# Attention and a rounded feed-forward block on one core: contexts 2 and 3 get a second place, the first weight unit comes in halves, zeros are multiplied at the top, and every engine's order is new

## The chip, the cores and the metric

The kernel runs on one core of a Trainium2 chip. The metric is the device time of one execution in microseconds. Before the change the median of three runs is 617.62 us (617.29 to 618.58).

## What is computed

There are 4 batches of 512 rows with 512 features each, and a context of 512 rows with 256 features for each batch. Attention weights are made of the context alone, and are applied to the layer-normed rows along their 512 features. Then a gated feed-forward block with 2048 hidden features follows, whose operands are rounded to FP8 values in blocks of 32 with a scale of their own.

```python
query = einsum('bnc,dc->bnd', ctx, Wq) + bq            # 4 x 512 x 128
key   = einsum('bnc,dc->bnd', ctx, Wk) + bk
attention = softmax(einsum('bnd,bmd->bnm', query, key))
x = x + einsum('bln,bmn->blm', layernorm(x), attention)
n = mx(layernorm(x))                                   # mx: per block of 32, scale * fp8(value / scale)
hidden = silu(n @ mx(gate_w).T) * (n @ mx(up_w).T)     # 2048 x 2048
x = x + mx(hidden) @ mx(down_w).T
```

## The kernel before

The kernel is written with one hand-ordered list of calls for each engine and semaphores between them. Sizes are cut as follows: the 2048 rows are 16 row tiles r of 128 (four to a batch b), the hidden features are 4 chunks c of 512, and the weights are 12 units u of 128x2048 floats. Units 2c and 2c+1 are gate and up of chunk c; units 8 to 11 are the down weights.

**Attention of a batch b.** `project(b, 0)` and `project(b, 1)` (L654) make query and key, four matmul records each. ScalarE copies them out (`take_projection`, L901). `energies(b, 0..3)` (L661) make the scores, VectorE takes each row's maximum (`row_max`, L1369), ScalarE the exponential (`exponential`, L927), VectorE the reciprocal of the sums (`row_sum`, L1374), ScalarE makes four diagonal matrices of them (`weigh`, L935). `turn_probs(b, 0..3)` (L668) turns and weighs the probabilities, ScalarE copies them out (`take_probs`, L942), `attend(b, 0..3)` (L677) applies them, and VectorE adds them to the rows (`add_attended`, L1386).

**Rows and weights.** VectorE and ScalarE round each unit and each batch of rows: `unit_reduce`, `unit_largest`, `unit_scale`, `unit_power`, `unit_magnitude` (ScalarE, L870), `unit_round` (two passes, L1350 and L1351) and `unit_dequant`, about five passes of 128x2048 on VectorE in all. The result is written as a high and a low half-precision part: `unit_hi` on ScalarE, a DMA of GpSimd that adds the high part to the negated value (`unit_rest`), `unit_lo` on ScalarE. Each part is turned by a DMA on SyncE's queue (`turn_unit_hi`, `turn_unit_lo`). Both parts lie in one buffer each, so a unit's part waits until that of the unit before is turned. The rows of a batch go the same way (`center`, `rows_scale`, `rows_round`, `rows_dequant`, `rows_hi`, `rows_lo`), and later each hidden row tile.

**Products.** `product(r, c)` (L693) needs the parts of units 2c and 2c+1 and those of its batch's rows: 24 matmuls, each 128x512. ScalarE applies silu to the gate (`silu_of`, L1000), VectorE multiplies (`hidden_of`, L1503). `down(r)` (L705, L708) is 48 matmuls. TensorE does 16 attends, 64 products and 16 downs, in an order given by its list and by the table `products`.

**Memory.** The table `bank_uses` says in which order each of the eight PSUM banks serves the results (p, e, t, a, g, u, d for projection, energies, turned, attended, gate, up, down): a result waits until its bank's former use is copied out. Before the change, contexts 2 and 3 are loaded over contexts 0 and 1 (`ctx[b % 2]`), so their loads wait for the projections. Centered rows of batch 0 go to `early_xw`, a slot of `h` that nothing uses before.

**SyncE's queue** issues the loads and the turning DMAs one after the other; a wait in it holds all that stand behind. Unit u+3 is loaded into the buffer of unit u once `unit_lo(u)` is done.

## Time and profile before

| | |
|---|---|
| median of three runs | 617.62 us |
| profiled execution, its own time | 618.75 us |
| its span | 617.0 us |
| TensorE busy | 599.0 us, 97% of the span |
| VectorE busy | 495.3 us, 80% |
| ScalarE busy | 301.9 us, 49% |
| first matmul | 8.46 us after the span's start |
| last matmul ends | about 613.1 us |

The profiled execution is 1.1 us above the median, and 1.75 us of its time lie around its span. A busy figure is the union of an engine's instructions; matmuls are pipelined, so a short gap between two groups can be hidden in it. The profile's granted clock is 1.00 in every slice but the last.

### The profile page before, as it was taken

Reading aid. Unit: us, or ns where it says so; the run is one execution under the profiler, and the core shown is the slowest. Engines: PE = TensorE matmul, PEld = TensorE weight load, DVE = VectorE, ACT = ScalarE, POOL = GpSimd, SP = SyncE. Lnnn points to the kernel's source line nnn. Section 1 sums busy time; section 2 is a strip of 40 time slices with the busy share of each in tenths; the row PEclk is TensorE's granted clock in tenths of the full one; section 3 lists DMA queues with packets and bytes.
Section 4 is the critical chain, followed back from the end, with each engine's and each line's share of the span. In section 5 each row is a group of like instructions: output and inputs, shape, how many; then the busy total and the mean of one; then the engine's idle time right before and its main releaser. Section 6 shows DMA issues by size and latency. Waiting matters only on the chain.

```text
span 617.0 us, 7089 instructions
## 1 busy us (share of the span) xinstructions
PE 599.0 (97%) x2624; PEld 276.9 (45%) x2624; DVE 495.3 (80%) x467; ACT 301.9 (49%) x449; POOL 42.4 (7%) x58
## 2 busy tenths in 40 slices
PE   4899989999999999999999999999999999999997
PEld 1535455444444444444444444444444444444443
DVE  5899999998999998996999999520149999999810
ACT  1899995645554545465455564502114232643420
POOL 1000000201000000101001110000000000010100
PEclk9999999999999999999999999999999999999999
DMA  8927769798987885968847758605000002777771
GB/s 336 410 76 168 223 191 261 176 266 211 204 223 199 209 211 141 217 120 170 205 95 155 158 110 185 119 1 85 1 1 1 2 0 37 134 122 134 122 135 34
DMA packets 147586, 90.18 MB, mean 146 GB/s; under 512 B 134240, under 2 KB 134368, under 8 KB 142816
## 3 DMA queue, kind: packets, MB, share of 16 engines
q1 hardware_dynamic: 142368, 63.78, 43.2%
q0 software_dynamic: 5184, 25.95, 18.7%
q8 instruction: 21, 0.34, 0.2%
q14 instruction: 13, 0.11, 0.0%
HBM read 25.76 MB, written 8.39 MB: 55 GB/s over the span
## 4 chain that ended last, share of the span: by engine, by line
PE 89%; ACT 6%; SPq 2%; DMA 2%; issue 1%; DVEq 0%; DVE 0%; ACTq 0%
PE bank L693 53%; PE bank L705 18%; PE bank L708 9%; PE bank L677 4%; PE bank L654 2%; ACT h L915 1%; PE bank L668 1%; ACT h L906 1%; PE bank L661 1%; DMA gu_hi<-in_ctxT 1%; SPq L377 1%; DMA xT<-hT 1%; ACT mag L870 1%; ACT hT L961 0%; ACT dn L927 0%
## 5 line engine op out<-in xcount | busy, mean ns | idle before, releaser
L693 PE MATMUL bank<-gu_hi,xT 128*128 128x512 f16 x1024 | 243.2, 379 | 0.4 <-DMA xT<-hT 0.4
L693 PEld LDWEIGHTS bank<-gu_hi,xT 128*128 128x128 f16 x1024 | 100.0, 98 | 121.8 <-DMA xT<-hT 1.1
L693 PE MATMUL bank<-gu_lo,xT 128*128 128x512 f16 x512 | 131.4, 379 | 0.0
L705 PE MATMUL bank<-dn,hT 128*128 128x512 f16 x512 | 113.1, 379 | 0.0
L1503 DVE SCALAR_TENSOR_TENSOR h<-bank,unscale,silu 128x512 f32<-128x512 f32 x64 | 46.5, 747 | 64.3 <-PE bank L693 60.4
L1000 ACT ACTIVATE silu<-bank,unscale 128x512 f32<-128x512 f32 x64 | 42.8, 682 | 102.8 <-PE bank L693 65.6
L705 PEld LDWEIGHTS bank<-dn,hT 128*128 128x128 f16 x512 | 50.1, 98 | 60.4
L693 PEld LDWEIGHTS bank<-gu_lo,xT 128*128 128x128 f16 x512 | 50.1, 98 | 60.4
L708 PE MATMUL bank<-dn,hT 128*128 128x512 f16 x256 | 57.9, 379 | 0.0
L677 PE MATMUL bank<-dn,h 128*128 128x512 f32 x128 | 55.7, 593 | 0.8 <-ACT dn L942 0.8
L1043 ACT ACTIVATE y<-bank,xnmr,odown 128x128 f32<-128x128 f32 x60 | 22.5, 456 | 52.6 <-PE bank L708 52.6
L1026 ACT ACTIVATE W<-h 128x2048 f16<-128x2048 f32 x16 | 30.6, 1910 | 31.8 <-DMA hT<-W 17.5
L1350 DVE SCALAR_TENSOR_TENSOR h<-mag,h 128x2048 f32<-128x2048 bf16 x18 | 41.2, 2287 | 4.3 <-ACT mag L870 4.3
L1351 DVE SCALAR_TENSOR_TENSOR h<-mag,h 128x2048 f32<-128x2048 bf16 x18 | 41.3, 2292 | 0.6
L870 ACT ACTIVATE mag<-h 128x2048 bf16<-128x2048 f32 x18 | 34.2, 1903 | 10.3 <-DVE h L1351 8.7
L894 ACT ACTIVATE hT<-W 128x2048 f16<-128x2048 f32 x12 | 22.9, 1908 | 32.3 <-DMA W<-hT 32.3
L708 PEld LDWEIGHTS bank<-dn,hT 128*128 128x128 f16 x256 | 25.1, 98 | 30.2
L677 PEld LDWEIGHTS bank<-dn,h 128*128 128x128 f32 x128 | 24.2, 190 | 30.8 <-issue 29.7
L1529 DVE TENSOR_TENSOR h<-h,hscale 128x2048 f32<-128x2048 f32 x16 | 36.6, 2290 | 1.5 <-ACT hscale L1008 1.1
L1517 DVE TENSOR_TENSOR h<-h,rscale 128x2048 f32<-128x2048 f32 x16 | 36.7, 2292 | 0.5
L1512 DVE TENSOR_REDUCE hscale<-h 128x64 f32<-128x2048 f32 x16 | 36.5, 2283 | 0.5
L1444 DVE TENSOR_REDUCE scale<-W 128x64 f32<-128x2048 f32 x12 | 27.3, 2276 | 7.2 <-DMA W<-in_units 7.2
(99 smaller groups left out, 534.8 us busy)
## 6 DMA issues: line engine op xcount, KB each, us to landing
W<-in_units SPq DMA_DIRECT2D x12, 1024.0 KB, 5.7
W<-hT POOLq DMA_DIRECT2D x12, 1024.0 KB, 5.9
h<-W POOLq DMA_DIRECT2D x6, 1024.0 KB, 6.2
h<-in_xcols SPq DMA_DIRECT2D x4, 1024.0 KB, 10.6
out_y<-y POOLq DMA_DIRECT2D x15, 256.0 KB, 4.9
gu_hi<-in_ctxT SPq DMA_DIRECT2D x4, 512.0 KB, 10.2
h<-in_xrows SPq DMA_DIRECT2D x2, 1024.0 KB, 15.1
out_y<-h SPq DMA_DIRECT2D x2, 1024.0 KB, 7.6
```

The source lines that it names most:

```text
L677: last = pe.matmul(bank[:, :], xTf[b % 2][:, j, lt * P:(lt + 1) * P], AT[:, j, :], start=(j == 0), stop=(j == HT - 1))
L693: last = pe.matmul(bank[:, :], xT[:, b % 2, part, k, :], w[:, c, g, j * 512:(j + 1) * 512], start=(j == 0 and not low), stop=(j == HT - 1 ...
L705: pe.matmul(bank[:, :], hT[:, r % 2, 0, k, :], dn[:, w, k, :], start=(k == 0 and w == 0), stop=False)
L708: last = pe.matmul(bank[:, :], hT[:, r % 2, 1, k, :], dn[:, 0, k, :], start=False, stop=(k == IT - 1))
L870: nc.scalar.activation(mag[:, :], v, ACT.Abs, scale=MAGIC).then_inc(mag_ready, 1)
L1000: nc.scalar.activation(silu[:, n % 2, :], bank_of(f"g{r}.{c}")[:, :], ACT.Silu, scale=unscale[:, 2 * c:2 * c + 1]).then_inc(silu_ready, 1)
L1350: then(dve.scalar_tensor_tensor(v, mag[:, :], floor, v, ALU.max, ALU.add))
L1351: dve.scalar_tensor_tensor(v, mag[:, :], floor, v, ALU.max, ALU.subtract).then_inc(mag_used, 1)
L1503: dve.scalar_tensor_tensor(hrow(r)[:, c * 512:(c + 1) * 512], bank_of(f"u{r}.{c}")[:, :], unscale[:, 2 * c + 1:2 * c + 2], silu[:, n % 2, ...
L1512: then(dve.tensor_reduce(s, blocks(row), AX.X, ALU.max, apply_absolute_value=True))
L1517: dve.tensor_tensor(blocks(row), blocks(row), each_block(rscale[:, :]), ALU.mult).then_inc(hv_ready, 1)
L1529: dve.tensor_tensor(blocks(row), blocks(row), each_block(hscale[:, r % 2, :]), ALU.mult).then_inc(hd_ready, 1)
```

## The change

**Places and loads.** Contexts 2 and 3 get a place of their own, the slot where batch 0's rows are centered later (`early_xw`). Their loads wait for nothing, and `center(0)` waits for all eight projections. Unit 0 is loaded by two DMAs of 128x1024, with a semaphore `half_in` for the first; VectorE takes the block maxima of each half as it comes. Context 0 is loaded ahead of the constants.

**TensorE's top.** VectorE clears a 128x512 half-precision tile, and TensorE multiplies it 18 times into bank 7 before it waits for the constants. Five matmuls of the 128x128 identity into bank `e0.0` stand between the projections and energies of batch 0. Nothing reads what either writes.

```diff
-        ctx = [ctx_all[:, n * 1024:(n + 1) * 1024].rearrange("p (t n) -> p t n", n=512) for n in range(2)]
+        ctx = [place[:, n * 1024:(n + 1) * 1024].rearrange("p (t n) -> p t n", n=512)
+               for place in (ctx_all, early_xw) for n in range(2)]
...
+            def load_half(u):
+                sp.dma_start(W[u][:, 0:UNIT // 2], units[u][:, 0:UNIT // 2]).then_inc(half_in, 16)
+
+            def load_rest(u):
+                sp.dma_start(W[u][:, UNIT // 2:], units[u][:, UNIT // 2:]).then_inc(w_in[u], 16)
...
-            load_unit(0)
+            load_half(0)
+            load_rest(0)
+            load_ctx(0)
             load_consts()
-            load_ctx(0)
             load_unit(1)
             load_unit(2)
+            load_ctx(3)
             load_ctx(1)
             load_columns(0)
             load_columns(1)
+            load_ctx(2)
             load_rows(0)
...
-            load_ctx(2)
-            load_ctx(3)
             sp.wait_ge(*unit_rest_in(0))
             turn_unit_hi(0)
...
             sp.wait_ge(*unit_rest_in(2))
+            turn_unit_lo(2)
+            sp.wait_ge(*unit_rest_in(3))
             turn_unit_hi(3)
-            turn_unit_lo(2)
-            load_unit(5)
+            turn_rows_hi(1)
+            turn_unit_lo(3)
             load_unit(6)
-            sp.wait_ge(*rows_rest_in(1))
-            turn_unit_lo(3)
-            turn_rows_lo(1)
-            turn_rows_hi(1)
             store_rows(3)
             sp.wait_ge(*unit_rest_in(4))
+            turn_rows_lo(1)
+            load_unit(7)
...
             def project(b, i):
-                pe.wait_ge(ctx_in[b % 2], 16 * (b // 2 + 1))
+                pe.wait_ge(ctx_in[b], 16)
...
+            keep_zeros(18)
             pe.wait_ge(consts_in, 32)
             project(0, 0)
             project(0, 1)
+            keep("e0.0", 5)
             energies(0, 0)
...
             def center(b):
+                if b == 0:
+                    dve.wait_ge(proj_ready, 2 * B)
...
+            dve.memset(zeros, 0.0).then_inc(zeros_ready, 1)
-            unit_reduce(0)
+            reduce_half(0)
+            reduce_rest(0)
```

**Orders.** The lists of all five engines, the tables `products` and `bank_uses` and the order of the roundings (`rounds`) are new. No product, attend, down or rounding is left out. The new `products` begins `(3, 0), (1, 0), (0, 0), (2, 0), (2, 1), (0, 1), (3, 1), (5, 0)`; before it began `(0, 0), (2, 0), (1, 0), (3, 0), (2, 1), (1, 1), (5, 0), (6, 0)`.

TensorE before, at the top: projections (L654), energies (L661) and turned probabilities (L668) of batches 0 and 1.

```order
1 L654 MATMUL bank<-gu_hi,gu_lo 128x512 [waits ctx_in0,consts_in]
2 L654 MATMUL bank<-gu_hi,gu_lo 128x512
3 L654 MATMUL bank<-gu_hi,gu_lo 128x512 [waits ctx_in0]
4 L654 MATMUL bank<-gu_hi,gu_lo 128x512
5 L661 MATMUL bank<-gu_lo 128x512 [waits qk_ready] x4
6 L654 MATMUL bank<-gu_hi,gu_lo 128x512 [waits ctx_in1]
```

TensorE now at the same place (L724 the zeros, L657 projections, L718 the identity, L664 energies).

```order
1 L724 MATMUL bank<-dn 128x512 [waits zeros_ready]
2 L724 MATMUL bank<-dn 128x512 x17
3 L657 MATMUL bank<-gu_hi,gu_lo 128x512 [waits ctx_in0,consts_in]
4 L657 MATMUL bank<-gu_hi,gu_lo 128x512
5 L657 MATMUL bank<-gu_hi,gu_lo 128x512 [waits ctx_in0]
6 L657 MATMUL bank<-gu_hi,gu_lo 128x512
7 L718 MATMUL bank<-gu_lo 128x128 x5
8 L664 MATMUL bank<-gu_lo 128x512 [waits qk_ready] x4
9 L657 MATMUL bank<-gu_hi,gu_lo 128x512 [waits ctx_in1]
```

The extra matmuls stand ahead of the first wait for data and in the wait for the copied projections. Further on, attends of batch 0 now come before the energies of batch 2, and the products (3, 0) and (1, 0) before the turned probabilities of batch 3.

ScalarE before, from the exponentials of batch 3 (L927) to its first silu (L1000); L870 is a magnitude, L894, L986 and L888 write parts, L935 is `weigh`, L942 `take_probs`, L961 the squares for batch 1's variances.

```order
63 L927 ACTIVATE dn,gu_lo<-bank,gu_lo 128x512 x2
64 L870 ACTIVATE mag<-W 128x2048
65 L894 ACTIVATE hT<-W 128x2048
66 L986 ACTIVATE hT<-h 128x2048
67 L888 ACTIVATE hT<-W 128x2048
68 L927 ACTIVATE dn,gu_lo<-bank,gu_lo 128x512 x2
69 L935 ACTIVATE h<-gu_lo 128x128 x4
70 L942 ACTIVATE dn<-bank 128x4x128 x4
71 L961 ACTIVATE hT,ysum<-h,nmean 128x512 x4
72 L973 ACTIVATE var<-ysum 128x4
73 L1000 ACT_TABLE_LOAD
74 L1000 ACTIVATE silu<-bank,unscale 128x512
```

ScalarE now at that place (L875 magnitude, L966 and L978 batch 1's variances, L1005 silu, L932 exponentials of batch 3, L940 `weigh`, L899 `unit_lo(2)`).

```order
62 L875 ACTIVATE mag<-W 128x2048
63 L966 ACTIVATE hT,ysum<-h,nmean 128x512 x4
64 L978 ACTIVATE var<-ysum 128x4
65 L1005 ACT_TABLE_LOAD
66 L1005 ACTIVATE silu<-bank,unscale 128x512
67 L883 ACTIVATE unscale<-pow 128x1
68 L885 ACTIVATE scale<-scale,rpow 128x64
69 L932 ACT_TABLE_LOAD
70 L932 ACTIVATE dn,gu_lo<-bank,gu_lo 128x512 x4
71 L1005 ACT_TABLE_LOAD
72 L1005 ACTIVATE silu<-bank,unscale 128x512
73 L940 ACTIVATE h<-gu_lo 128x128 x4
```

Two silus and three table loads now stand ahead of `weigh(3, 0)`, and so do the squares for batch 1, which before came behind all of batch 3's softmax. Those squares are written where the turned parts of batch 0's rows lie, so they wait until both are turned.

VectorE now, around `row_sum(3)` (L1379); L1424 ends `rows_scale(1)`, L1391 is `add_attended(2, 3)`, L1451 `unit_reduce(4)`, L1520 `hidden_of`.

```order
74 L1424 TENSOR_TENSOR h<-h,rscale 128x2048
75 L1391 SCALAR_TENSOR_TENSOR dn,ysum<-bank,gu_lo,dn 128x512
76 L1451 TENSOR_REDUCE scale<-W 128x64
77 L1379 RECIPROCAL gu_lo<-gu_lo 128x4
78 L1468 TENSOR_SCALAR scale<-scale 128x64
79 L1470 TENSOR_REDUCE smax<-scale 128x1
80 L1520 SCALAR_TENSOR_TENSOR h<-bank,unscale,silu 128x512
81 L1355 SCALAR_TENSOR_TENSOR W<-mag,W 128x2048
```

`row_sum(3)` waits for the four exponentials of the block above; the rounding of unit 3 (L1355), which before came ahead of the low part of batch 0's rows, now comes behind it.

## Rows read from the trace of the kernel before

**Rows 1.** The page: busy time by engine, and the chain's shares by engine.

```profile
span 617.0 us, 7089 instructions
...
PE 599.0 (97%) x2624; PEld 276.9 (45%) x2624; DVE 495.3 (80%) x467; ACT 301.9 (49%) x449; POOL 42.4 (7%) x58
...
PE 89%; ACT 6%; SPq 2%; DMA 2%; issue 1%; DVEq 0%; DVE 0%; ACTq 0%
```

**Rows 2.** TensorE's waits: line, releaser, us in total, times, longest.

```profile
PE bank L654 <- DMA gu_hi<-in_ctxT: 8.5, 1, 8.5
PE bank L668 <- ACT h L935: 2.1, 2, 1.2
PE bank L661 <- ACT gu_lo L901: 2.1, 2, 1.3
PE bank L677 <- ACT dn L942: 0.8, 1, 0.8
PE bank L693 <- DMA xT<-hT: 0.4, 1, 0.4
```

**Rows 3.** Chain of waits in order of time: start us, us, what.

```profile
8.46 6.64 PE bank L654 x8
...
19.57 3.45 PE bank L654 x8
...
57.34 3.58 PE bank L668 x32
...
98.90 4.65 DMA xT<-hT
...
107.23 13.73 PE bank L677 x32
120.96 155.40 PE bank L693 x720
```

**Rows 4.** Stretches: busy of PE, PEld, DVE, ACT, POOL, granted clock, DMA share, GB/s.

```profile
0.00:7.50 7.50, 0.00 (x0) 0.00 (x0) 1.77 (x1) 1.28 (x1) 0.35 (x7) 1.00 0.72 253
0.00:21.60 21.60, 12.36 (x22) 5.12 (x23) 12.02 (x13) 8.06 (x15) 1.78 (x8) 1.00 0.93 355
0.00:24.00 24.00, 13.76 (x24) 5.45 (x24) 14.35 (x18) 9.43 (x18) 2.13 (x9) 1.00 0.94 363
```

**Rows 5.** Timeline of VectorE and ScalarE: start us, us, instruction, idle before.

```profile
5.73 2.29 DVE L1444 TENSOR_REDUCE scale<-W 128x64 f32<-128x2048 f32 x1 [5.73 <-DMA W<-in_units]
...
12.32 0.69 ACT L901 ACTIVATE gu_lo<-bank,gu_lo 128x512 f32<-128x512 f32 x1 [10.16 <-PE bank L654]
...
16.05 1.90 ACT L870 ACTIVATE mag<-W 128x2048 bf16<-128x2048 f32 x1
...
61.50 0.71 ACT L961 ACTIVATE hT<-h,nmean 128x512 f32<-128x512 f32 x1
...
106.62 0.21 ACT L973 ACTIVATE var<-ysum 128x4 f32<-128x4 f32 x1
106.84 1.28 ACT L1000 ACT_TABLE_LOAD   x1
108.14 0.69 ACT L1000 ACTIVATE silu<-bank,unscale 128x512 f32<-128x512 f32 x1
```

**Rows 6.** Groups of instructions: count, busy us, mean ns, idle before.

```profile
L927 ACT ACTIVATE dn<-bank,gu_lo 128x512 f32<-128x512 f32 x16 | 10.9, 682 | 0.2
```

**Rows 7.** Timeline of SyncE's queue: start us, us of issue, DMA.

```profile
56.05 5.32 SPq L372 DMA_TRANSPOSE gu_hi<-hT  x1
...
94.28 1.89 SPq L372 DMA_TRANSPOSE gu_hi<-hT  x1
...
130.71 3.69 SPq L377 DMA_TRANSPOSE gu_lo<-hT  x1
...
270.07 15.40 SPq L408 DMA_TRANSPOSE hT<-W  x2
...
298.66 2.56 SPq L394 DMA_TRANSPOSE xT<-W  x1
```

**Rows 8.** The same columns as rows 4, for VectorE's fullest stretches.

```profile
130.00:160.00 30.00, 30.00 (x141) 13.58 (x139) 26.30 (x34) 15.11 (x15) 3.67 (x4) 1.00 0.94 235
160.00:190.00 30.00, 30.00 (x141) 13.62 (x139) 28.63 (x27) 15.60 (x15) 2.44 (x4) 1.00 0.85 202
...
250.00:276.00 26.00, 26.00 (x123) 11.75 (x121) 24.61 (x24) 13.74 (x20) 2.79 (x3) 1.00 0.78 163
```

More of the change, by code:

```diff
@@ L767, in _ @@
             turn_probs(2, 3)
+            attend(1, 2)
+            energies(3, 0)
+            attend(1, 3)
+            energies(3, 1)
+            energies(3, 2)
+            energies(3, 3)
             attend(2, 0)
@@ L853, in _ @@
             down(9)
+            product(15, 2)
+            product(15, 3)
             down(10)
@@ L1274, in _ @@
+            hidden_magnitude(11)
             silu_of(14, 1)
@@ L1644, in _ @@
-            unit_largest(7)
-            hidden_of(5, 0)
-            hidden_of(6, 0)
-            unit_power(7)
-            unit_scale(7)
-            hidden_of(0, 1)
+            unit_scale(4)
+            add_attended(3, 2)
+            unit_reduce(5)
+            unit_round(4)
+            add_attended(3, 3)
+            unit_dequant(4)
+            unit_reduce(6)
+            unit_largest(5)
+            unit_largest(6)
+            unit_scale(5)
+            unit_scale(6)
+            unit_round(5)
@@ new lines, in _ @@
+            hidden_dequant(9)
+            hidden_of(10, 2)
+            hidden_lo(9)
+            hidden_of(10, 3)
+            hidden_scale(10)
+            hidden_of(13, 0)
+            hidden_scale(11)
+            hidden_round(10)
+            hidden_of(15, 0)
+            hidden_of(14, 0)
+            hidden_dequant(10)
+            hidden_of(14, 1)
+            hidden_round(11)
+            hidden_dequant(11)
+            hidden_of(14, 2)
+            hidden_of(14, 3)
+            hidden_of(12, 0)
```

722 lines of the change are left out of this document (347 added, 375 removed), and 10 rows, old and new, of the table products.

## The prediction, on record before the changed kernel was run

> **What bounds the kernel now.** The page comes first: TensorE is busy for 599.0 of 617.0 us, and 89% of the chain of waits is its own work [rows 1]. Its list of waits says where the rest is: it stands still for 8.5 us at the top until context 0 is in, and for 5.4 us in seven short waits, all before 104 us [rows 2]. Then the chain: from 120.96 us on TensorE runs without a stop [rows 3]. So a gain can come only from the first 121 us, or be lost behind them.
>
> The size of that stretch is read from the chain [rows 3]. The first eight projection records take 6.64 us and the next eight 3.45, about two to one: TensorE ran them at the lower of its two levels (1.2 against 2.4 GHz), after having stood idle since the start, though the granted clock of the profile reads 1.00 there [rows 4]. That costs 3.2 us. At the faster pace the attention's work is 4 x 3.45 for projections, the same for energies (equally many records of the same shape), 4 x 3.58 for the turned probabilities and 4 x 13.73 for the attends, together 96.8; a product is 155.40 x 24 / 720 = 5.18. From the first matmul to 120.96 are 112.5 us, and the work in it is 96.8 + 5.2 = 102.0. **10.5 us are lost there**: 3.2 to the slow clock, 7.3 to waits (the 5.4 of the list and small ones between groups that pipelined ends hide).
>
> **The change, part by part.** The sum is made against the profiled execution (618.75), and the difference is then taken off the median, 1.1 below it.
>
> *The start.* TensorE still waits for half of unit 0, its rest, context 0 and the constants: 1024 + 512 + 321 KB are 1.90 MB, the very bytes that were ahead of it before, and by 7.5 us the DMA engines had moved 7.5 x 253 = 1.90 MB [rows 4]. One issue more on SyncE and the smaller consts as the last could cost 0.5 us, the idle first microseconds of the engines exclude a gain beyond 0.5. I take 0.
>
> *The zeros.* A product's matmul takes 5.18 / 24 = 0.216 us at the quick pace, so 0.43 at the slow one. Eighteen like it are 18 x 0.43 = 7.7 us if all are slow, and run from about 1.2 us, when VectorE can have cleared the tile, to 8.1 (the last ones quick) or 8.9. Before, the pace doubled at the end of 6.6 us of work [rows 3], so the last zeros and all projections should be quick: **-3.2**. The row bounds it from both sides: 0 if zeros or their place don't raise the clock, -3.4 if all of it goes.
>
> *The first gap.* Before, energies followed 0.8 us after the projections. Now ScalarE does `unit_magnitude(0)` (1.90) between the two copies (0.69 each) [rows 5]: from the first copy's start, 1.73 after TensorE's, 0.7 + 1.85 + 0.7 = 3.2 us pass, against 1.72 that TensorE has in its second projection. The gap is 1.5 us, and the five identity matmuls (5 x 3.58/16 = 1.1 us) lie in it. Cost: **+1.5** (0.8 to 2). In return the magnitude is out of the way. VectorE, whose first reduction began at 5.73 us with the whole unit [rows 5], does half of it before that, and its reductions of units 1 and 2 fill what was a wait.
>
> *The other early waits.* The exponentials of batch 0 start when its energies do, 2.5 us earlier than before. While ScalarE works on them TensorE has projections of batches 1, 2 and 3, since contexts 2 and 3 wait for no one. What is late next is the loads: units 0 to 2, the constants, four contexts and two columns are 7.7 MB, moved by 21.6 us (21.6 x 355), and rows 0 come at 24.0 x 363 = 8.7 MB [rows 4]; with about 1 us to land, ScalarE wants context 2's projection at 22 and rows 0 at 23. Walking both lists on from there with the durations of rows 3, 5 and 6, each later bank and copy comes 0 to 0.3 us behind TensorE. I take **+0.8** in place of what the seven waits cost (0 to 2). The attends of batch 0 then begin near 34.6 us instead of 43.4, and product (3, 0) near 90.4.
>
> *Its operands.* The product needs the parts of units 0 and 1 and of batch 0's rows. Before, VectorE rounded unit 3 before it wrote the rows' low part; now that comes after, which is what brings the low part forward. By the walk VectorE ends it at about 82, ScalarE `unit_lo(1)` too. SyncE's queue then holds four turnings at 1.9 to 3.7 us each, and the last takes 4.65 to land [rows 3, 7]: 91.5, and it is first needed 1.7 us into the product, at 92.1. I cost it at nothing; with one issue of 5.3 us as the longest row it is +2.8.
>
> *Softmax of batch 3.* This is the term that I trust least. ScalarE holds, behind the low part's turning at 91.5: four squares (4 x 0.71) and the variance, a table load and silu (1.28 + 0.6), the rescale 0.3, a table load (1.3), four exponentials of 0.86 each with their accumulator (0.682 alone [rows 6]), a table load and silu (1.9), and `weigh` [rows 5]. That ends at 103.3. TensorE has done products (3, 0) and (1, 0) at 90.4 + 10.4 = 100.8. So `turn_probs(3, 0)` waits **+2.6** (0.5 where squares need not wait for the turning, 4.5 with a late turning). VectorE meets the same knot: `row_sum(3)` stands ahead of `hidden_of(3, 0)` and `unit_round(3)`, and it idles some 3 us, off TensorE's path at first.
>
> The Trainium skill, ScalarE: Activation LUTs, section What ACT_TABLE_LOAD costs, gives about 1.28 us for the load and 1.38 us of drain, 2.66 for each switch. This trace has the 1.28, but silu starts 1.30 us after the load's start, and the load 0.01 after the instruction before it, so no drain is seen [rows 5]. By the page the three loads cost 4.1 us more, and the wait would be 6.7.
>
> *After that* the walk finds attends of batch 3 ending near 126, with two more products done than at 120.96. Lost: 1.5 + 0.8 + 2.6 = 4.9 against 10.5, so **-5.6**.
>
> *The long middle.* TensorE's work to the end is the same, so the 5.6 us stay if all that it needs is 5.6 us earlier too. VectorE is the engine to ask: 26.3 to 28.6 of each 30 us are busy [rows 8]. It gains by the start and the order some 4 us up to 95 and loses 2 to 3 of them at `row_sum(3)`; between 130 and 276 it idled about 10 us, a part of it for products that now come earlier. Walking its list to the rounding of hidden tile 0 I get 4.4 us earlier than before. The slack before: hidden tile 0's high part was issued at 270.07 [rows 7] and takes about 4.7 us to land, 1.6 before `down(0)` at 276.36; batch 2's low part at 298.66 [rows 7] + 4.65 was 0.7 ahead of its use. So 5.6 earlier is just out of reach: **+1.0** (0 to 4).
>
> *The tail.* Product (15, 3) now ends with six downs behind it instead of ten, 6 x 10.36 = 62 us. VectorE's remaining work behind it is about 18 us, so each hidden part is still ready when its buffer is free; nothing changes.
>
> **Sum**: -3.2 + (1.5 + 0.8 + 2.6 - 7.3) + 1.0 = -4.6 us. 618.75 becomes 614.15, and the median 617.62 becomes **613.0**.
>
> **The rivals.** Differences that a measurement can tell from none are 0.2%, 1.2 us: faster is under 616.4, slower over 618.9.
>
> *Knot loosened.* ScalarE reaches the exponentials of batch 3 in time and the middle follows: only 1.5 + 0.8 are lost, -8.2 at most, and 0.6 late: about 610.0. For: every wait of the walk is a few tenths. Against: the squares stand behind a DMA.
>
> *VectorE holds the middle.* It gains only 2 us by 276 us, and TensorE waits for units and hidden tiles until it is only that far ahead: 617.6 - 2.0 = 615.6. For: 95% busy [rows 8]. Against: it idled there for products.
>
> *The clock stays low.* Zeros don't raise it, or not before the projections: 613.0 + 3.2 = 616.2.
>
> *Table switches with drain.* By the page's price, as a mechanism a wait of 6.7 us at `turn_probs(3, 0)`: 613.0 + 4.1 = 617.1, no change. The rows speak against it.
>
> *SyncE's queue, slower.* `turn_unit_hi(3)` now waits for unit 3's rest, and high part, rows' high part and `unit_lo(3)`'s turning follow it. By the walk the last lands at 129.5, needed at about 131.5 by product (2, 1). Turnings took 1.9 to 5.3 us to issue [rows 7]. If the queue is 6.6 us or more late there, all gain is gone: TensorE waits 4.6 us; at 9 us late the time is 613.0 + 7 = 620, since units 4 to 7 go through the same queue. Against: before, the same four turnings had a similar margin and nobody waited.
>
> **How the numbers follow.** Forecast, 611.3 to 615.0: 0.50. Knot loosened, 609.3 to 611.3: 0.15. VectorE, 615.0 to 616.8: 0.15. Clock low: 0.05. Table drain: 0.05. Queue: 0.10. Faster takes the first two, most of the third and half of the fourth: 0.82. Same: 0.08. Slower: 0.10. The range 610.0 to 617.0 leaves out about 0.1 on the slow side and 0.08 on the fast.
>
> **What would show it.** Right: zeros from about 1.2 us and projections of 3.45 us for eight records; TensorE at the attends of batch 0 near 35 and at product (3, 0) near 90; a wait of 2 to 3 us before the turned probabilities of batch 3, released by ScalarE; the end of the attends at 126. Wrong: projections of 6.6 us; a wait of TensorE for a turning DMA in product (3, 0), (2, 1) or (5, 0), or for hidden tile 0 before `down(0)`; waits of over 1 us behind 130 us in sum would fell the term for the middle.

## The result, and the profile after

The changed kernel takes 622.34 us (median of 6 runs, 621.61 to 625.34), the kernel before 618.26 in the same session (6 runs): a ratio of 1.0074, 95% interval 1.0052 to 1.0096. It is slower by 4.1 us where 4.6 us less were forecast. The profiled execution is the fastest of the six, 621.61 us with a span of 619.8, and that of the kernel before, 618.75, lies 0.5 above its median: the traces differ by 2.8 us of span and show that much of the 4.1.

The page of the changed kernel, the lines that answer to [rows 1]:

```profile
span 619.8 us, 7149 instructions
...
PE 605.6 (98%) x2652; PEld 279.5 (45%) x2652; DVE 495.0 (80%) x469; ACT 303.7 (49%) x451; POOL 44.6 (7%) x58
...
PE 63%; DMA 16%; ACT 6%; SPq 5%; DVE 4%; issue 4%; DVEq 0%; ACTq 0%; POOLq 0%
```

The busy time of TensorE grew by the zeros and by matmuls at half pace. The last line says where to look: before, 89% of the chain was TensorE's own work, now 63%, with 16% for DMAs and 5% for SyncE's queue. The chain runs through the queues for a long stretch. TensorE's timeline, start, us and the idle time before each group, shows where it waits (these rows answer to [rows 2]):

```profile
1.18 6.73 PE L724 MATMUL bank<-dn 128*128 128x512 f16 x18 [1.18 <-DVE dn L1564]
8.82 3.70 PE L657 MATMUL bank<-gu_hi,gu_lo 128*128 128x512 f32 x8 [0.92 <-DMA gu_lo<-in_consts]
14.03 3.70 PE L664 MATMUL bank<-gu_lo 128*128 128x512 f32 x8 [0.39 <-ACT gu_lo L906]
...
35.58 13.90 PE L680 MATMUL bank<-dn,h 128*128 128x512 f32 x32
...
102.81 3.81 PE L671 MATMUL bank<-h,dn 128*128 128x128 f32 x32 [1.40 <-ACT h L940]
...
255.64 1.86 PE L696 MATMUL bank<-gu_hi,xT 128*128 128x512 f16 x4 [5.38 <-DVE h L1520]
257.30 1.91 PE L696 MATMUL bank<-gu_lo,xT 128*128 128x512 f16 x4
...
278.45 7.07 PE L708 MATMUL bank<-dn,hT 128*128 128x512 f16 x32 [0.18 <-issue]
...
306.71 1.90 PE L696 MATMUL bank<-gu_hi,xT 128*128 128x512 f16 x8 [0.43 <-DMA xT<-W]
```

The early waits are short: the first 125 us came out as forecast. The attends of batch 3 end at 125.36 with three products done, where before, in the same view, they ended at 120.80 with one (the chain of [rows 3] has 120.96); two products are 10.36 us, so TensorE is 5.80 us ahead there. With 28 products left (28 x 5.18 = 145.04) `down(0)` would start at 270.4. It starts at 278.45, so 8.05 us are lost between. 5.38 are the wait before product (7, 0), 1.75 the half pace behind it (16 matmuls in 5.20 us and not 3.45), 0.42 two short waits, and 0.5 is listed nowhere: at each of the three waits the group before it reaches 0.17 us into it. Less the lead of 5.80, `down(0)` is 2.25 us late (276.20 before). The wait is for `hidden_of(1, 2)`, which stands behind tile 0's rounding on VectorE. That rounding starts at 247.89 us, before at 246.14. The granted clock by stretch (columns of [rows 4]):

```profile
240.00:250.00 10.00, 10.00 (x48) 4.46 (x46) 8.50 (x4) 5.74 (x4) 0.00 (x0) 1.00 0.80 177
250.00:255.00 5.00, 0.26 (x2) 0.00 (x0) 4.93 (x4) 0.13 (x1) 0.00 (x0) 0.74 1.12 253
255.00:260.00 5.00, 4.36 (x13) 1.63 (x14) 4.86 (x7) 2.93 (x3) 1.76 (x2) 0.58 0.58 139
260.00:270.00 10.00, 10.00 (x48) 4.58 (x47) 8.60 (x13) 7.53 (x11) 0.00 (x0) 1.00 0.85 205
```

From product (8, 0) on the two kernels are alike: 314.9 us to the end before (302.10 to 617.0), 315.4 after (304.38 to 619.8). Everything is decided by then.

VectorE's waits between 90 and 250 us say where its lead went. Before, then after (us in total, times, longest):

```profile
DVE scale L1444 <- DMA W<-in_units: 1.5, 2, 0.8
```

```profile
DVE scale L1451 <- DMA W<-in_units: 11.5, 6, 3.3
```

It now waits for weight units. A unit is loaded when the low part of the third before it has been made. The chain of waits of the changed kernel, as the profile infers it, says what leads to product (7, 0), where before it was TensorE alone from 120.96 us on (L318 loads a unit, L383 turns a low part, `DMA dn<-hT` is a turning until it lands, `DMA W<-hT` a rest until it lands, L893 makes a high part):

```profile
213.65 0.83 SPq L318
...
214.64 5.31 SPq L383
...
220.11 4.34 DMA dn<-hT
...
224.73 5.81 DMA W<-hT
...
230.64 1.92 ACT hT L893
...
232.94 6.12 DMA W<-hT
...
239.08 1.77 SPq L383
...
241.44 4.52 DMA dn<-hT
...
245.99 1.81 ACT mag L875
...
247.89 2.30 DVE h L1355
...
254.75 0.76 DVE h L1520
...
255.64 22.62 PE bank L696 x96
```

So the load of unit 11, the turned low part 8, the turned high part 9, the rests of 9 and 10, and then tile 0's magnitude and rounding follow one another. SyncE's issue of the turned low parts gives each unit's time (start, us of issue; the changed kernel):

```profile
145.08 0.72 SPq L318 DMA_DIRECT2D W<-in_units  x1
145.84 5.42 SPq L383 DMA_TRANSPOSE gu_lo<-hT  x1
...
181.60 5.83 SPq L383 DMA_TRANSPOSE gu_lo<-hT  x1
200.03 1.94 SPq L383 DMA_TRANSPOSE gu_lo<-hT  x1
...
239.08 1.77 SPq L383 DMA_TRANSPOSE dn<-hT  x1
...
271.96 16.78 SPq L414 DMA_TRANSPOSE hT<-W  x2
```

All issues of turned low parts, with the last one, the high part of hidden tile 0, for which `down(0)` waits (for comparison two runs told of below):

```
low part of unit     4      5      6      7      8      9      10     11     tile 0, high
before             152.05 165.52 181.18 197.00 212.07 226.36 243.75 263.96  270.07
after              145.84 166.11 181.60 200.03 214.64 239.08 246.65 266.21  271.96
loads ahead        151.18 167.82 182.50 198.54 213.66 229.09 246.53 266.88  273.02
rests behind       150.44 163.90 179.58 199.42 213.07 233.88 249.49 270.55  276.68
```

Unit 4 is 6.2 us early, unit 5 is 0.6 late, unit 9 is 12.7 late; 4 of those 12.7 are a wait for unit 10's rest (e5, below). Unit 7 shows one loss alone: its high part is made 3.5 us earlier than before (182.85 against 186.38), its low part 3.0 later (198.05 against 195.07), and between them stands its rest, now behind the turning. So the question for the experiments is whether VectorE's order at 250 us costs the time, or this chain of rests and turnings.

### The profile page after: what moved, and what is told of

Read it like the earlier page. It is cut to its first block, busy times and chain, and to the rows that moved or that the text cites. A ratio compares the mean times of both kernels' runs of the same rounds, so it can differ in the third digit from the quotient of the medians.

```text
span 619.8 us, 7149 instructions
## 1 busy us (share of the span) xinstructions
PE 605.6 (98%) x2652; PEld 279.5 (45%) x2652; DVE 495.0 (80%) x469; ACT 303.7 (49%) x451; POOL 44.6 (7%) x58
## 4 chain that ended last, share of the span: by engine, by line
PE 63%; DMA 16%; ACT 6%; SPq 5%; DVE 4%; issue 4%; DVEq 0%; ACTq 0%; POOLq 0%
PE bank L696 31%; PE bank L708 17%; PE bank L711 8%; DMA W<-hT 7%; PE bank L680 3%; SPq L383 3%; DMA h<-in_ctxT 2%; PE bank L671 2%; ACT hT L893 1%; DMA dn<-hT 1%; DMA gu_hi<-hT 1%; PE bank L657 1%; DVE W L1492 1%; DMA W<-in_units 1%; DMA W<-W 1%
## 5 line engine op out<-in xcount | busy, mean ns | idle before, releaser
L1520 DVE SCALAR_TENSOR_TENSOR h<-bank,unscale,silu 128x512 f32<-128x512 f32 x64 | 46.9, 746 | 49.5 <-PE bank L696 45.0
L1005 ACT ACTIVATE silu<-bank,unscale 128x512 f32<-128x512 f32 x64 | 43.0, 681 | 84.4 <-PE bank L696 54.5
L875 ACT ACTIVATE mag<-h 128x2048 bf16<-128x2048 f32 x18 | 34.3, 1903 | 27.7 <-DVE h L1356 18.4
L1355 DVE SCALAR_TENSOR_TENSOR h<-mag,h 128x2048 f32<-128x2048 bf16 x18 | 41.2, 2289 | 3.7 <-ACT mag L875 3.6
L1552 DVE SCALAR_TENSOR_TENSOR W<-h,W 128x2048 f16<-128x2048 f32 x10 | 22.9, 2288 | 18.6 <-DMA hT<-W 16.8
L899 ACT ACTIVATE hT<-W 128x2048 f16<-128x2048 f32 x12 | 22.9, 1908 | 25.7 <-DMA W<-hT 21.8
```

The lines of the kernel that those rows point to most:

```text
L875: nc.scalar.activation(mag[:, :], v, ACT.Abs, scale=MAGIC).then_inc(mag_ready, 1)
L1005: nc.scalar.activation(silu[:, n % 2, :], bank_of(f"g{r}.{c}")[:, :], ACT.Silu, scale=unscale[:, 2 * c:2 * c + 1]).then_inc(silu_ready, 1)
L1355: then(dve.scalar_tensor_tensor(v, mag[:, :], floor, v, ALU.max, ALU.add))
L1520: dve.scalar_tensor_tensor(hrow(r)[:, c * 512:(c + 1) * 512], bank_of(f"u{r}.{c}")[:, :], unscale[:, 2 * c + 1:2 * c + 2], silu[:, n % 2, ...
```

## First experiments: the order at 250 us, and the start

**e1**: the two elementwise steps for which TensorE waited go ahead of tile 0. (In the kernel before only the first of them, `hidden_of(1, 2)`, stood there.)

```
-            hidden_round(0)
-            hidden_dequant(0)
             hidden_of(1, 2)
             hidden_of(1, 3)
+            hidden_round(0)
+            hidden_dequant(0)
```

> The changed kernel (622.3 us) with one edit: VectorE does hidden_of(1, 2) and hidden_of(1, 3) before hidden_round(0) and hidden_dequant(0), as the kernel before did. Theory A (one place in one order): TensorE's wait of 5.4 us before product (7, 0) and the slow clock behind it, together 7 to 8 us, go and nothing takes their place, so about 615. Theory B (the chain of the units and of hidden tile 0 is what is late): the wait moves to down(0), which can't start before about 277 us because hidden tile 0's parts are turned no earlier; then 620.5 to 621.5, with a wait of 4 to 6 us in front of down(0).

Measured: 622.62 us, ratio 1.0075 (1.0056 to 1.0095), no change, and just over what theory B gave. The wait was replaced by others, two of them for silus and not the one before `down(0)` that B named:

```profile
260.09 1.86 PE L696 MATMUL bank<-gu_hi,xT 128*128 128x512 f16 x4 [3.14 <-ACT silu L1005]
274.18 1.02 PE L696 MATMUL bank<-gu_hi,xT 128*128 128x512 f16 x4 [1.90 <-ACT silu L1005]
280.84 7.07 PE L708 MATMUL bank<-dn,hT 128*128 128x512 f16 x32 [1.32 <-issue]
```

**e4** adds `hidden_magnitude(0)` ahead of `unit_lo(10)` on ScalarE.

> As e1_h12_first, and ScalarE does hidden_magnitude(0) ahead of unit_lo(10), which waits for unit 9's low part to be turned. VectorE then rounds hidden tile 0 without its wait of 1.4 us. Theory A: as e1, 615. Theory B: down(0) comes 0 to 1.5 us earlier than in e1, since behind the rounding unit 11's low part and the turnings are also waited for: 619.5 to 621.

Measured: 624.87 us, 1.0106 (1.0084 to 1.0127). TensorE stands 5.53 us at 275.47 for a silu behind `unit_lo(11)`: `unit_lo(10)` starts at 248.11 and not 246.66, `unit_lo(11)` at 266.31 and not 265.03, and `down(0)` at 283.42 and not 280.84. A low part made later delays what follows it; the time is over both theories.

**e2** is the changed kernel without the 18 zeros and the 5 identity matmuls.

> The changed kernel without the 18 zero matmuls and without the 5 identity matmuls; all else is kept. The projections of batch 0 should take 6.6 us instead of 3.5 again. Theory B (the place that sets the time in the middle is fed by loads, VectorE and DMAs, not by TensorE): nothing of that is lost at the end, 622 to 623, and the wait before product (7, 0) is 2 to 3 us shorter. Rival (TensorE's start carries through to the end): 625.5.

Measured: 625.60 us, 1.0118 (1.0101 to 1.0135), 3.3 over the changed kernel. Its projections take 5.47 us for eight and the wait before product (7, 0) grows to 7.70. The number is the rival's (TensorE's start carries through), and it agrees with the 3.2 us forecast for the zeros; the way there is another. The eight projections lose 1.8 us, TensorE is 2.2 late at batch 3's turned probabilities (105.01 against 102.81), and the wait before product (7, 0) adds 2.3: tile 0's chain is later too (low part 10 at 252.05 and not 246.65). No run shows why.

**e3** is the kernel before with the zeros alone.

> The kernel before with one addition: VectorE clears the tile first and TensorE multiplies it 18 times before it waits for the constants. If the 3.2 us of the slow clock are TensorE's and the middle has room, 615.0. If units and hidden tiles stay where they were, TensorE can only be earlier by the slack that was there, 1.3 us at down(0) and 0.8 at batch 2's rows: 616.8 to 617.6, with waits of 2 us in all behind 130 us.

Measured: 619.98 us (10 runs, 618.40 to 621.66), 1.0031 (1.0016 to 1.0046). 1.7 us slower, where both theories had it faster. The profiled execution is the fastest of the ten, 618.40, so its trace does not show why the median rose; it shows where the zeros' gain goes. TensorE leads by 3.05 us at the first energies, by 0.13 at context 2, which is loaded late, by 1.68 at the attends of batch 0 (before, other waits stood there) and by 0.38 at product (8, 0).

```profile
31.39 5.39 PE L654 MATMUL bank<-gu_hi,gu_lo 128*128 128x512 f32 x12 [3.04 <-DMA gu_hi<-in_ctxT]
...
301.72 1.04 PE L693 MATMUL bank<-gu_hi,xT 128*128 128x512 f16 x4 [0.95 <-DMA xT<-W]
```

**e7** takes that wait away: contexts 2 and 3 have the places of the change and are loaded early, all other orders are those of before.

> The kernel before with the 18 zero products and the early contexts alone: contexts 2 and 3 go to the later place of the centered rows and are loaded behind the columns and behind rows 1, center(0) waits for all projections; all other orders stay those of before. Theory A (the early gain is real and only the new orders behind it lose it): the wait of 3.04 us for context 2 of the run with zeros alone is gone, the attends of batch 0 start at 39.5 to 40.5 us, product (0,0) is reached 3 us earlier than before the change, and 615.5 to 617 us come out. Theory B (the middle is held by the chain of units and VectorE, whatever the start): attends earlier by the same, but TensorE waits again for turned rows and units from 100 us on, until it is at most 1 us ahead: 617.5 to 618.5 us.

Measured: 618.33 us, 1.0002 (0.9991 to 1.0012), as theory B had it. The attends start at 41.77, as in e3: the wait for context 2 is gone and one of 1.15 us for ScalarE and one of 1.34 stand in its place. `down(0)` starts at 275.01 (276.20 before), but product (8, 0) waits 0.72 us and starts at 301.79 (302.10). What lead there is in this execution is lost before 302 us in the old order too, in front of rows 2. How much of it the zeros made is not sure, since the start varies between executions of the same top. Without zeros, in the kernel before and in e10, e14 and e11 (all told of below), the eight projections took 6.63, 5.81, 5.29 and 5.11 us, and the attends started at 43.45, 42.33, 42.30 and 41.70; with zeros (e3, e7, e13) the projections took 3.67 us and the attends started at 41.77, 41.77 and 41.54.

**e5** and **e8** mend one place of SyncE's list each: low part 9 waits for its own rest and not for unit 10's; unit 4's high part is turned before its low part.

```
             turn_unit_hi(9)
-            sp.wait_ge(*unit_rest_in(10))
+            sp.wait_ge(*unit_rest_in(9))
             turn_unit_lo(9)
             turn_unit_hi(10)
             reload_rows(2)
+            sp.wait_ge(*unit_rest_in(10))
             turn_unit_lo(10)
```

> The changed kernel with one place of SyncE's list altered: the turning of unit 9's low part waits for the rest of unit 9 and no longer for that of unit 10, which is waited for after the reload, as in the kernel before. Theory A (the place of that wait makes the late middle): the turning is issued at about 235 us and not at 239, unit_lo(10) and hidden_magnitude(0) come 2 to 4 us earlier, the wait of 5.4 us before product (7,0) shrinks by about 1.5 us and with it the slow clock: about 620 us. Theory B (the chain of units ahead sets the times, and low part 10 waits for its own rest): the turning moves by 4 us, but unit_lo(10) by less than 1 us and the wait stays over 4.5 us: 622.3 us.

> The changed kernel with the turnings of unit 4 swapped on SyncE: high part first, then low part, as before the change. GpSimd's rest of unit 5 waits for the high part. Theory A (the lead of 6 us that unit 4's low part has at 146 us is lost in this place): the rest of unit 5 starts 3 to 5 us earlier, low part 5 is made at about 162 us and not 166, and the units behind keep 2 us or more of it; the wait before product (7,0) falls below 3.5 us: about 619.5 us. Theory B (units 6 to 11 are held by the weight buffers and their loads): low part 5 comes earlier, low parts 9 to 11 by less than 1 us, the wait stays near 5 us: 622 us.

Measured: 621.75 us, 1.0054 (1.0035 to 1.0073), and 622.40 us, 1.0063 (1.0042 to 1.0083); waits of 5.33 and 5.22 us before product (7, 0). Neither place is the cause. e5 shows why:

```profile
235.08 5.65 SPq L383 DMA_TRANSPOSE dn<-hT  x1
```

Low part 9 is issued 4 us earlier, beside the rest of unit 10 (added from 233.60 on), and takes 5.65 us to issue and not 1.77. `unit_lo(10)`, which needs it landed, starts at 244.21 as it did (244.08). In e8 the rest of unit 5 still started at 158.16 (158.41 in the changed kernel), since its high part was made only then: VectorE does `unit_reduce(7)`, which waits 3.17 us for its load (3.25 in the changed kernel), ahead of `unit_dequant(5)`.

**e6** puts e1 and e5 together and moves four silus up on ScalarE, two ahead of `hidden_hi(0)`, one ahead of `unit_lo(11)`, one ahead of `attended_variances(2)`.

> The changed kernel with the orders around hidden tile 0 mended together: hidden_of(1,2) and (1,3) ahead of hidden_round(0) on VectorE, the turning of unit 9's low part behind its own rest on SyncE, and on ScalarE silu (4,2) and (5,3) ahead of hidden_hi(0), silu (4,3) ahead of unit_lo(11) and silu (7,0) ahead of attended_variances(2). Theory A (only the orders at 235 to 275 us lose the time): TensorE has no wait over 0.5 us between 208 us and down(0), which starts at 276 to 277, since hidden tile 0 lands there; no slow clock: 619.5 to 620.5 us. Theory B (the units' chain is as late as before the change, and VectorE passes its lateness on whatever the order): waits of 2 us or more stay in that stretch, in other places: 621.5 to 623 us.

Measured: 623.36 us, 1.0079 (1.0060 to 1.0098). This is the run that settles the first question:

```profile
261.61 1.02 PE L697 MATMUL bank<-gu_hi,xT 128*128 128x512 f16 x4 [0.89 <-DVE h L1521]
...
277.68 9.82 PE L709 MATMUL bank<-dn,hT 128*128 128x512 f16 x32 [5.55 <-issue]
```

TensorE has no long wait for VectorE any more, has done its products by 272.1 us, and then stands for 5.55 us until hidden tile 0 has landed (its high part is issued at 272.25). Wherever the order at 250 us puts the wait, the tile comes no earlier. Theory A of these runs falls.

## The chain of rests and turnings

A unit goes through: high part made (ScalarE), rest added (GpSimd's DMA), low part made, both turned (SyncE). Two moves of the change in it were each made alone in the kernel before: the loads of units 7, 9 and 11 stand ahead of the turned low parts 4, 6 and 8, and the rests of units 7 and 9 start behind the turning of their own high part. The change moved more there: low part 4 is turned ahead of high part 4, the rest of unit 5 follows the turned high part 4, low part 9 is turned behind unit 10's rest, and `unit_lo(9)` stands behind `unit_hi(10)`.

**e10**, the loads (and likewise 9 and 11):

```
             turn_unit_hi(4)
-            turn_unit_lo(4)
             load_unit(7)
+            turn_unit_lo(4)
```

> The kernel before with one part of the change alone: units 7, 9 and 11 are loaded ahead of the turning of low parts 4, 6 and 8 on SyncE. Theory A (a turning right behind a load takes 5.3 us to issue, since it waits until the load has gone, against 2.0 to 2.5): low parts 4, 6, 8 land 3 us later, each rest behind them starts up to 3 us later, hidden tile 0 comes 1 to 3 us later and the time grows by 1 to 2.5 us: 619.5 to 620.5. Theory B (the chain has that slack, VectorE sets the pace): 618.2, no change.

Measured: 623.67 us (4 runs, 622.29 to 627.46), 1.0102 (1.0065 to 1.0138); profiled 622.29, 3.5 over before.

```profile
151.18 5.45 SPq L377 DMA_TRANSPOSE gu_lo<-hT  x1
...
278.04 8.75 PE L705 MATMUL bank<-dn,hT 128*128 128x512 f16 x32 [2.20 <-issue]
```

The issue of the turning grows from 2.04 to 5.45 us, and from unit 5 on the low parts fall behind by 1 to 3 us (third row of the table). That is more than theory A gave: by the medians 5.6 us.

**e11**, the rests (and likewise 9, with 144 and 160 on GpSimd):

```
-            sp.wait_ge(*unit_rest_in(7))
             turn_unit_hi(7)
+            sp.wait_ge(*unit_rest_in(7))
...
-            pool.wait_ge(wT_in[1], 112)
+            pool.wait_ge(wT_in[0], 128)
             unit_rest(7)
```

> The kernel before with another part of the change alone: the rests of units 7 and 9 are added behind the turning of their own high part and not ahead of it (SyncE's wait and GpSimd's wait). Theory A (this serial step is what loses the units' lead): low parts 7 and 9 are made 4 to 6 us later, low part 11 and hidden tile 0 by 2 to 4 us, TensorE stands 2 to 4 us before down(0) or (7,0): 620.5 to 622.5 us. Theory B (VectorE sets the pace and the step has slack): low parts 7 and 9 later, low part 11 by less than 1 us: 618 to 618.8 us.

Measured: 627.16 us (4 runs, 625.54 to 627.37), 1.0143 (1.0126 to 1.0159), the largest effect of all, and more than theory A gave it. GpSimd's rest of unit 9 before, then in this run, and what TensorE does:

```profile
217.56 0.87 POOL L553 DMA_DIRECT2D W<-hT  x1 [8.89 <-ACT hT L888]
```

```profile
226.04 0.88 POOL L553 DMA_DIRECT2D W<-hT  x1 [15.37 <-DMA dn<-hT]
...
281.72 9.96 PE L705 MATMUL bank<-dn,hT 128*128 128x512 f16 x32 [6.12 <-issue]
```

The sum closes: `down(0)` starts 281.72 - 276.20 = 5.5 us late and its first 32 matmuls take 9.96 and not 7.07, together 8.4; the span is 625.4 - 617.0 = 8.4 longer. So both moves cost time by themselves, the one 3.5 and the other 8.4 us in profiled executions, 5.56 and 9.05 by the medians of one session. The serial chain sets hidden tile 0 in the kernel before as well, with a slack of about 1.1 us: the tile's high part is issued 2.95 and 6.61 us later and `down(0)` starts 1.84 and 5.52 later.

Two runs put the chain of before back into the changed kernel, on top of e6 (`unit_lo(9)` ahead of `unit_hi(10)` and `unit_dequant(5)` ahead of `unit_reduce(7)` with it). **e9** has the loads where before had them, **e12** where the change has them.

> The changed kernel with the mended orders of the run before, and the units' chain of the kernel before: on SyncE and GpSimd units 4 to 11 in the order of before (rest, high part turned, low part turned, then the load of the next unit), on ScalarE unit_lo(9) ahead of unit_hi(10), on VectorE unit_dequant(5) ahead of unit_reduce(7). In the run with mended orders alone TensorE stood 5.55 us in front of down(0), because the high part of hidden tile 0 was issued at 272.25 us, behind low part 10 at 246.68 and low part 11 at 266.50, and that goes back to the rest of unit 9, which now starts behind its own turning and landed at 230.7 against 224.3 us. Theory A (the place of the rests in the chain loses the lead): low part 9 is made at 225 us or earlier, low part 11 turned by 262 to 264, down(0) starts at 273 to 276 us, and 617 to 618.5 us come out. Theory B (VectorE has no more lead than before whatever the queues do, and the later loads cost it): low part 11 at 266 us again, down(0) at 277 us or later: 621 to 623 us.

> The same as the run with the units' chain as before, but units 7, 9 and 11 are loaded ahead of the turnings of units 4, 6 and 8, as in the changed kernel. What differs between the two is only whether a load stands in front of a turning in SyncE's queue. Theory A (a turning behind a load takes 5.3 us to issue, and its later landing costs more than the earlier load gives): 0.5 to 1.5 us slower than its twin. Theory B (VectorE waits for loads in this kernel, 11 us in sum, so an earlier load is worth more): 1 to 2 us faster than its twin, and VectorE's waits for loads sum to less than half of the twin's.

Measured: e9 625.92 us, 1.0132 (1.0106 to 1.0158); e12 622.95 us, 1.0073 (1.0056 to 1.0090). e9 lies above both of its theories. Undoing the queue's part alone does not undo the loss. e12 says it of the rests: it has those of units 5, 7 and 9 where before had them, and takes as long as e6 (1.0073 against 1.0079), so in the changed kernel their place alone is not shown to cost what it costs in e11. VectorE's new list asks for units 7, 9 and 11 earlier than the old one, and with the loads later it waits 14.5 us for them in e9, 8.9 in e12. Of the pair, theory B had the direction (an early load is worth more to this list, 3.0 us), though the waits did not fall to less than half: the queue's order has to be judged together with VectorE's list.

**e14** takes a load out from in front of a turning in the kernel before: the reload of rows 2 goes behind low part 10 and high part 11. **e13** does it in e7. **e15** adds to e13 that the rest of unit 10 is ahead of its high part's turning. **e16** does both, and the same for unit 9, in e6, with `unit_lo(9)` ahead of `unit_hi(10)`. The edit of e15 in this place:

```
-            turn_unit_hi(10)
-            reload_rows(2)
             sp.wait_ge(*unit_rest_in(10))
+            turn_unit_hi(10)
             turn_unit_lo(10)
             turn_unit_hi(11)
+            reload_rows(2)
...
-            pool.wait_ge(wT_in[0], 176)
+            pool.wait_ge(wT_in[1], 160)
             unit_rest(10)
```

> The kernel before with one move on SyncE: the reload of rows 2 stands behind the turnings of low part 10 and high part 11 and not ahead of them. There the turning behind the reload takes 5.05 us to issue. Theory A (the chain of turnings sets hidden tile 0): low part 10 takes 2 to 3 us to issue, the rest of unit 11 starts 2 to 3 us earlier, hidden tile 0's high part is issued at 267 to 268 us and not 270.07. TensorE gains little by it, as it stood only in front of nothing there: 617 to 618 us, down(0) where the products end. Theory B (VectorE holds hidden tile 0): issue at 270 us again, 618.2 us.

> The kernel before with zeros, early contexts and the reload of rows 2 behind the two turnings, all other orders as before. With the early gain but the old reload, down(0) came at 275.0 us and rows 2 were 0.7 us late at 301.8. Theory A: hidden tile 0 and rows 2 come 2 us earlier, no wait of TensorE over 0.3 us behind 104 us, 615.5 to 617 us. Theory B: down(0) and the wait in front of product (8,0) as they were, 618.3 us.

> The run with contexts and reload, and besides the rest of unit 10 is added behind low part 9's turning and ahead of high part 10's own, as units 5 to 9 have it, which takes one serial turning out of the chain. Theory A: low part 10 is made 2 to 3 us earlier again, the rest of unit 11 starts as soon as its high part is made and turned, and the time is that of its twin less 0 to 1 us, since TensorE has no wait left there: 615 to 616.5 us. Theory B: no change against the twin.

> The changed kernel with mended orders (the run where TensorE stood 5.55 us before down(0)), and the end of the units' chain shortened: rests of units 9 and 10 ahead of their own high parts' turning, unit_lo(9) ahead of unit_hi(10), the reload of rows 2 behind high part 11. Theory A: low part 9 is made at 226 to 229 us, hidden tile 0's high part issued at 267 to 269 and not 272.25, the wait before down(0) falls to 1 us or less and with it the slow clock: 617 to 619 us. Theory B (VectorE has lost the lead to loads before that): the wait stays over 3 us: 621 to 623 us.

Measured:

```
        us       ratio (95%)                high part of tile 0   down(0)   wait before (8,0)
e14   617.99   0.9997 (0.9987 to 1.0007)    268.73              275.06    none
e13   618.22   1.0000 (0.9991 to 1.0010)    268.60              274.75    0.94
e15   617.48   0.9992 (0.9982 to 1.0001)    266.79              274.42    0.59
e16   620.75   1.0046 (1.0032 to 1.0060)    269.83              275.27    none
```

e15's time is not told from that of the kernel before, and e13 and e15 miss the gain that their theory A had. e16 confirms the chain in the changed kernel, by four moves together: against e6 the tile's issue is 2.4 us earlier, `down(0)` 2.4 us, and the median 2.6 us. TensorE still stands 4.00 us there, more than the 1 us expected of theory A, and the time lies between the two theories; 2.5 us stay against before. In e14 the turned low part 10 took 1.32 us to issue and not 5.05, and the tile came 1.3 us earlier in the trace, but that execution was 1.1 us ahead at the attends of batch 0 already; the time did not move. e13 to e15 show the next link: with the tile early, rows 2 are late.

**e17** fills the 4 us in e16 with 16 matmuls on weights, whose result `down(0)` overwrites (`hidden_of(4, 3)` goes up to free their bank).

> The changed kernel with the chain shortened (the run that stood 4.00 us before down(0)), with 16 matmuls on weights put before down(0), whose result is overwritten by down(0), and hidden_of(4,3) ahead of hidden_round(1), so that their bank is free. Theory A (the slow clock is a price of its own behind each wait): down(0) starts where it did, at 275 us, within 0.5, but its 32 matmuls take 7.1 us and not 8.75, and the time falls by 1 to 1.7 us, to 619.0 to 619.8. Theory B (the half pace is no matter of the wait, or tile 0's chain is itself slower with a busy TensorE): 8.75 us again, 620.8 us.

Measured: 620.99 us, 1.0056 (1.0038 to 1.0074), no change against e16, and neither theory as written.

```profile
271.50 3.62 PE L719 MATMUL bank<-gu_hi 128*128 128x512 f16 x16
275.48 7.07 PE L710 MATMUL bank<-dn,hT 128*128 128x512 f16 x32 [0.36 <-issue]
...
302.88 1.04 PE L698 MATMUL bank<-gu_hi,xT 128*128 128x512 f16 x4 [1.34 <-DMA xT<-W]
```

The clock part of theory A is right: `down(0)` takes 7.07 and not 8.75 us, and `down(1)` starts 1.5 us earlier. But product (8, 0) starts at 302.88 against 302.85. Rows 2 do not come earlier, so the 1.5 us turn into a wait.

**e18** goes after rows 2 in e15: tile 0's high part is turned ahead of its low part, since `hidden_hi(1)` waits for it, and `rows_hi(2)` is made ahead of `take_down(0)`.

```
-            turn_hidden_lo(0)
             turn_hidden_hi(0)
+            turn_hidden_lo(0)
...
-            take_down(0)
             rows_hi(2)
+            take_down(0)
```

> The kernel before with zeros, early contexts, reload and rest of unit 10 as in the run of 617.5 us, and two moves more: SyncE turns hidden tile 0's high part ahead of its low part, and ScalarE makes rows_hi(2) ahead of take_down(0). Theory A (serial chain: high part 0 landed, hidden_hi(1), rest, low part 1 turned, rest of rows 2, turned rows): hidden_hi(1) starts 1.5 to 2 us earlier, at 271.7 to 272, the turned low part of rows 2 is issued at 295 to 295.5 and not 296.94, the wait of 0.59 us before product (8,0) is gone: 616.6 to 617.2 us. Theory B (rows 2 are held by VectorE's rounding): issue at 296.9 and a wait of 0.6 us as before, 617.5 us.

Measured: 617.06 us (11 runs), ratio 0.9982 (0.9974 to 0.9991): 1.2 us faster than before and 5.3 than the changed kernel, the only run that is faster than the kernel before beyond its interval. That it is faster than e15 is not shown: the intervals overlap. The time is the one that theory A gave, the way is not. `hidden_hi(1)` starts at 269.83 and not 273.54, more than expected, but low part 2 of the rows is issued at 296.95 as in e15 (296.94), and product (8, 0) starts at 301.16 (301.07). GpSimd has `add_out(0)` first, which waits for `take_down(0)`. The rest of rows 2 still starts 1.5 us earlier than in e15, but right behind `add_out(0)` it takes 7.35 us to land and not 5.84:

```profile
287.09 0.88 POOL L567 DMA_DIRECT2D out_y<-y  x1 [13.67 <-ACT y L1043]
287.65 1.20 POOL L556 DMA_DIRECT2D W<-W  x1
```

## Why the prediction was wrong

*The start*: right in its mechanism. Zeros from 1.18 us, eight projections in 3.70 us (3.54 to the next group), the first gap 1.67 us (1.5 forecast) with the identity matmuls in it, attends of batch 0 at 35.58 (34.6 forecast), product (3, 0) at 90.89 (90.4). The first projection starts 0.36 us later than before, where 0 was taken. The 3.2 us of the zeros were read from one execution, the slowest at its top of those recorded: 5.11 to 6.63 us against 3.67 make 1.4 to 3.0. The list of [rows 2] has six short waits, not seven; the sum of 5.4 is right.

*Softmax of batch 3*: the mechanism was right, a wait released by ScalarE, 1.40 us and not 2.6. ScalarE at that place (start, us):

```profile
93.96 1.28 ACT L1005 ACT_TABLE_LOAD   x1
95.25 0.69 ACT L1005 ACTIVATE silu<-bank,unscale 128x512 f32<-128x512 f32 x1
...
96.29 1.28 ACT L932 ACT_TABLE_LOAD   x1
97.58 0.69 ACT L932 ACTIVATE dn<-bank,gu_lo 128x512 f32<-128x512 f32 x1
```

Each switch costs 1.29 us, load to next instruction. The drain of 1.38 us that the Trainium skill (ScalarE: Activation LUTs, What ACT_TABLE_LOAD costs) adds to a switch does not show here either, and the rival built on it has fallen.

*After that*: attends end at 125.36 (126 forecast), and 5.80 us were won against 5.6. The early sum held against this execution of the kernel before; against one with a quicker start it would be 1 to 2 us less.

*The long middle*: here the prediction failed. The term was +1.0 (0 to 4) and it measured +8.05 to `down(0)`, 0.4 more behind it. The step that failed is "Walking its list to the rounding of hidden tile 0 I get 4.4 us earlier". VectorE starts that rounding 1.75 us later than before (247.89 against 246.14). The walk added up VectorE's work and took its loads as there; it waited 11.5 us for them, and 1.5 before. The loads hang on low parts, and these on a serial chain through GpSimd and SyncE, whose order the change altered between units 4 and 10. The prediction looked at that queue only as far as unit 3 and took it for safe because "nobody waited"; e10 and e11 show that each of the two later moves, alone in the kernel before, costs 3.5 and 8.4 us of span, and the chain of the changed kernel runs through both. How the 8.05 divide between the moves and VectorE's list is not shown. It also left out where `hidden_of(1, 2)` stands; by e1 and e6 that was no cause, only the place of the wait.

*The slow clock* was costed at the top and nowhere else. Behind the wait of 5.38 us it cost 1.75.

*The rivals*: "VectorE holds the middle" had the right engine standing late and 615.6 us, as it left 2 us of the lead. Only "SyncE's queue, slower" let the lead turn into a loss (620), by the right queue and with the wrong place: unit 3's low part is issued at 124.93 us, and 4.65 more give the 129.5 of the walk. *The tail*: right, 314.9 and 315.4 us.

What stays open: 2.5 us between e16 and the kernel before. VectorE still waits 10.7 us for loads in e16; that its list costs them is argued, not shown. No run puts VectorE's new list into the kernel before or the old one into the changed kernel, and e12 leaves open what the place of the rests costs there. The Trainium skill (DMA: Bandwidth & Descriptors, Rules for kernel authors) says, where it speaks of which DMAs must wait for each other, that a transpose next to ordinary DMAs needs nothing. As a rule on data no run speaks against it. It gives no time, and the rows show one: 5.45 and 5.65 us of issue beside a load or a rest against 2.04 and 1.77 alone. A chain in which rests and turnings run side by side throughout was not tried.

## What to carry to other kernels

A gain at the start is worth what the last resource in the middle lets through: before counting it, follow one item of the pipeline (here a weight unit) through every queue that it passes, with its waits and issue times, and not only the busiest engine's sum of work. Where an order is changed, walk each serial handover that the diff touches, and look at what the chain runs through. Its shares by engine say where to look, not what it costs: TensorE has 89% in the kernel before and 63% in the changed kernel, but 68% in e18, the fastest of all, and 74% in e11, the slowest. When mending one place only moves a wait, the cause is upstream, and putting single moves of the change into the kernel before shows which of them cost time there. One profiled execution is also a thin base for a term of 1 to 3 us: its start may be a late one.

## What was not expected of the hardware

A turning issued right behind a load of 1 MB, or while a rest is being added, took 5 us or more to issue (5.42, 5.83, 5.45, 5.65 above) against 1.3 to 3.7 for most others. The longer waits of TensorE before `down(0)` were followed by matmuls at half pace; the first 32 take 7.07 us without a wait:

```
wait before down(0), us     0.38   1.32   2.20   3.62   4.00   5.51   5.55   6.12
first 32 matmuls, us        7.07   7.07   8.75   8.75   8.75   9.40   9.82   9.96
run                         e7     e1     e10    e9     e16    e12    e6     e11
```

So such a wait costs up to 2.9 us more than its length, and matmuls without use in it take that away (e17). Its length alone does not decide it: 2.27 us in e2, before batch 3's turned probabilities, and 3.04 in e3, before context 2's projections, were followed by matmuls at full pace (3.81 us for 32, 5.39 for 12; granted clock 1.00), while 2.33 in e9, at the same place as in e2, brought 5.44 us and a clock of 0.58. No run here shows what decides.
